# Edge one-hot columns with the block as the innermost dimension, read by TensorE with a step

## The reference, cut to what matters

```python
def _L0_gnn_ref(x, rots, idx_i, idx_j):        # rots: 100000 angles, idx_j sorted
    def step(mat, t):                           # one rotation of two rows, in order
        i, j, theta = t
        c, s = cos(theta), sin(theta)
        mat = mat.at[i].set(c * mat[i] - s * mat[j])
        mat = mat.at[j].set(s * mat[i] + c * mat[j])   # both from the rows before
    m = scan(step, eye(256), (idx_i, idx_j, rots)).T
    return x @ m

xn = _layernorm(x)                              # x: 6250 x 256
x = x + _L0_gnn_ref(xn, edge_weight, src, dst) + _L0_mix_ref(xn[None], ...)[0]
x = x + _L0_ffn_ref(_layernorm(x)[None], ...)[0]    # 8 experts, the best 2 per row
```

## Time and profile before

| | |
|---|---|
| median of 3 runs | 734.21 us (733.88 to 734.66) |
| the profiled execution's own time | 737.21 us |
| its span, first to last instruction | 735.3 us |
| busy: PE, PEld | 644.6 us (88%), 551.3 us (75%) |
| busy: DVE, ACT, POOL | 472.9 us (64%), 449.9 us (61%), 388.6 us (53%) |
| mean granted TensorE clock | 0.928 |

### The profile page before, as it was taken

The page is one execution under the profiler, slowest core; times in us unless marked ns, Lnnn a source line. Parts: engine busy times, 40 slices in busy tenths (PEclk is TensorE's granted clock), DMA queues, the critical chain, the costliest instruction groups (busy, mean ns, idle before and its releaser), DMA issues.

```text
span 735.3 us, 18134 instructions
## 1 busy us (share of the span) xinstructions
PE 644.6 (88%) x4079; PEld 551.3 (75%) x4080; DVE 472.9 (64%) x1877; ACT 449.9 (61%) x1235; POOL 388.6 (53%) x532
## 2 busy tenths in 40 slices
PE   5789899754798998059999999899989999999996
PEld 4457577532687776048998999899979999999996
DVE  5797666699865799333544444344457777777775
ACT  6777666487234699336665666566656666666663
POOL 6104777145434177715776777323246656666554
PEclk8899999955599999569999999999999999999999
DMA  8830112246400477622443334222223333333332
GB/s 241 229 88 12 22 31 23 52 142 203 142 27 2 125 225 218 199 71 95 140 138 123 120 119 131 70 69 62 69 79 103 101 98 103 106 102 96 107 97 69
DMA packets 60873, 78.10 MB, mean 106 GB/s; under 512 B 15868, under 2 KB 49488, under 8 KB 60570
## 3 DMA queue, kind: packets, MB, share of 16 engines
q1 hardware_dynamic: 45703, 42.94, 21.0%
q0 software_dynamic: 14544, 34.11, 13.9%
q10 hardware_dynamic: 576, 0.54, 0.3%
HBM read 47.53 MB, written 31.53 MB: 108 GB/s over the span
## 4 chain that ended last, share of the span: by engine, by line
PE 67%; DVE 9%; issue 7%; DMA 5%; POOL 4%; ACT 4%; SPq 2%; DVEq 0%; POOLq 0%; ACTq 0%
PE banks L2716 22%; PE banks L2726 20%; PE banks L2324 5%; PE banks L2668 5%; PE banks L2303 4%; POOL send_d L903 3%; PE banks L2707 3%; DMA R<-in_edge_weight_dram 1%; DMA R<-send_d 1%; DMA out_dram<-R,dest_now 1%; PE banks L2314 1%; DVE R L1760 1%; PE banks L2429 1%; PE banks L2294 1%; PE banks L2419 1%
## 5 line engine op out<-in xcount | busy, mean ns | idle before, releaser
L2716 PE MATMUL banks<-R 128*128 128x128 f32 x1696 | 210.4, 278 | 3.6 <-ACT R L1288 3.5
L2716 PEld LDWEIGHTS banks<-R 128*128 128x128 f32 x1696 | 201.1, 194 | 4.6 <-ACT R L1288 4.5
L2726 PE MATMUL banks<-R 128*128 x848 | 200.4, 379 | 0.0
L1301 ACT ACTIVATE R<-banks,b1c 128x128 f32<-128x128 f32 x424 | 142.9, 363 | 54.2 <-PE banks L2716 53.8
L2726 PEld LDWEIGHTS banks<-R 128*128 128x128 f32 x848 | 153.1, 191 | 16.4
L1288 ACT ACTIVATE R<-banks,bet_c,gam_c 128x128 f32<-128x128 f32 x212 | 85.4, 453 | 114.8 <-PE banks L2707 112.3
L2211 DVE COPY R<-R 128x1024 f32 x106 | 74.3, 701 | 77.6 <-PE banks L2716 59.8
L903 POOL DMA_INDIRECT send_d<-R,slot_all x98 | 98.5, 1005 | 45.7 <-issue 40.6
L916 POOL DMA_INDIRECT first_d<-R,dest_now x54 | 61.0, 1130 | 94.4 <-DVE R L2216 79.4
L925 POOL DMA_INDIRECT R<-first_d,get_now x52 | 53.7, 1033 | 48.9 <-DVE get_now L2193 46.8
L916 POOL DMA_INDIRECT out_dram<-R,dest_now x52 | 63.3, 1217 | 29.8 <-issue 26.5
(11 more groups left out here) (553 smaller groups left out, 957.0 us busy)
## 6 DMA issues: line engine op xcount, KB each, us to landing
R<-send_d SPq DMA_DIRECT2D x106, 131.0 KB
R<-in_L_ffn_W_dram SPq DMA_DIRECT2D x16, 512.0 KB, 4.5
R<-in_x_dram SPq DMA_DIRECT2D x14, 512.0 KB, 4.6
R<-in_x_dram SPq DMA_DIRECT2D x5, 1024.0 KB, 12.4
send_d<-zrow SPq DMA_DIRECT2D x14, 131.0 KB, 5.2
send_d<-R,slot_all POOLq DMA_INDIRECT x98
erec_d<-R SPq DMA_DIRECT2D x1, 1400.0 KB
R<-in_L_ffn_b_dram SPq DMA_DIRECT2D x1, 1024.0 KB, 5.6
```

The costliest lines, as they stand in the source:

```text
L1301: last = nc.scalar.activation(hT[b][:, c, :], bank[2 + 2 * b + c // 2][:, (c % 2) * P:(c % 2 + 1) * P], ACT.Gelu, bias=b1c[:, bass.ds(e, 1 ...
L2716: last = mm(bank[2 + 2 * b + c // 2][:, (c % 2) * P:(c % 2 + 1) * P], w1c[b][:, kb, c * P:(c + 1) * P], xmT[b][:, kb * P:(kb + 1) * P], st ...
L2726: last = mm(bank[6 + b][:, 0:D], hT[b][:, c, :], w2s[:, bass.ds(e, 1), c, :].rearrange("p a h -> p (a h)"), start=(c == 0), stop=(c == H / ...
```

## The change

The one-hot columns are laid out with the block innermost, for each number a run of 26 (or 24) blocks, where before there was for each block a run of 128 (or 33) numbers. The first half now has 26 blocks and the second 24, where both had 25. POOL makes a constant `numbers16` of 128 x 26 bf16 on 125 partitions, which holds each number 26 times, in place of the row of 128; it is made at the same place of POOL's list by one copy from `col0` that reads each element 26 times. In the compares the blocks' ends are now read with a step of 1 innermost (and again for each number), and so are the constant and the output. The count of elements compared is as before. The matmuls read their operands with a step: for one block, 128 stationary columns and 33 (or 9) moving columns at a step of 26 elements (first half), 24 (second half) or 5 (head). The constant lies in R3, where the carving of the later tiles moves up by 1664 words; `col16` is gone from R1.

```diff
-        col16 = R1[0:EP, NT * D:NT * D + P // 2].bitcast(BF16)
+        numbers16 = prep(P, PB // 2 + PB // 2 % 2, dt=BF16, parts=EP)
...
-        half_c = PB // 2
+        half_c = PB // 2 + PB // 2 % 2
+        blocks_in = (half_c, PB - half_c)
...
         def cut_of(v, at, n, m):
-            return v[:, at:at + (n * m + 1) // 2].bitcast(BF16)[:, 0:n * m].rearrange("p (c n) -> p c n", c=n)
+            return v[:, at:at + (n * m + 1) // 2].bitcast(BF16)[:, 0:n * m].rearrange("p (n c) -> p n c", c=n)
...
-        hist_lo = [cut_of(t, 0, half_c, P) for t in tails]
-        hist_hi = [cut_of(t, at_hi, half_c, RC) for t in tails]
+        hist_lo = [cut_of(t, 0, m, P) for t, m in zip(tails, blocks_in)]
+        hist_hi = [cut_of(t, at_hi, m, RC) for t, m in zip(tails, blocks_in)]
...
-        def by_block(v, c0, c1, n, parts=EP):
-
-            return v[0:parts, c0:c1].rearrange("p (c a) -> p c a", a=1).broadcast_to([parts, c1 - c0, n])
...
-            link(nc.gpsimd.tensor_copy(col16[:, :], col0[0:EP, 0:P]))
+            link(nc.gpsimd.tensor_copy(numbers16, col0[0:EP, 0:P].rearrange("p (n c) -> p n c", c=1).broadcast_to([EP, P, half_c])))
...
             def hist_columns(h):
-                TT(hist_lo[h], by_block(ends_lo, h * half_c, (h + 1) * half_c, P), over_tiles(col16[0:EP, 0:P], half_c), ALU.is_equal).then_inc(S["edge_dve"], 1)
+                TT(hist_lo[h], over_tiles(ends_lo[:, h * half_c:h * half_c + blocks_in[h]], P), numbers16[:, :, 0:blocks_in[h]], ALU.is_equal).then_inc(S["edge_dve"], 1)
 
             def hist_rows():
                 for h in range(2):
-                    TT(hist_hi[h], by_block(ends_hi16, h * half_c, (h + 1) * half_c, RC), over_tiles(col16[0:EP, 0:RC], half_c), ALU.is_equal)
-                TT(head_lo, by_block(ends_lo, PB, PB + PH, P, HP), over_tiles(col16[0:HP, 0:P], PH), ALU.is_equal)
-                TT(head_hi, by_block(ends_hi16, PB, PB + PH, HC, HP), over_tiles(col16[0:HP, 0:HC], PH), ALU.is_equal).then_inc(S["edge_dve"], 1)
+                    TT(hist_hi[h], over_tiles(ends_hi16[:, h * half_c:h * half_c + blocks_in[h]], RC), numbers16[:, 0:RC, 0:blocks_in[h]], ALU.is_equal)
+                TT(head_lo, over_tiles(ends_lo[0:HP, PB:PB + PH], P), numbers16[0:HP, :, 0:PH], ALU.is_equal)
+                TT(head_hi, over_tiles(ends_hi16[0:HP, PB:PB + PH], HC), numbers16[0:HP, 0:HC, 0:PH], ALU.is_equal).then_inc(S["edge_dve"], 1)
...
                 for c in range(PH):
-                    mm(misc[:, P:P + HC], head_lo[:, c, :], head_hi[:, c, :], start=(c == 0), stop=(c == PH - 1))
+                    mm(misc[:, P:P + HC], head_lo[:, :, c], head_hi[:, :, c], start=(c == 0), stop=(c == PH - 1))
                 for c in range(PB):
-                    last = mm(misc[:, P + HC:P + NCH], hist_lo[c // half_c][:, c % half_c, :], hist_hi[c // half_c][:, c % half_c, :],
+                    last = mm(misc[:, P + HC:P + NCH], hist_lo[c // half_c][:, :, c % half_c], hist_hi[c // half_c][:, :, c % half_c],
                               start=(c == 0), stop=(c == PB - 1))
```

## The result

The changed kernel took 738.93 us in the median (737.7 to 741.28, 5 runs) against 734.21 us (732.23 to 734.66, 5 runs): +4.7 us between the medians. As a ratio it is 1.0069, 95% interval 1.0053 to 1.0086, which is +5.1 us (3.9 to 6.3). Slower was the forecast, with +1.8 us; the second interval reaches down to that, the first lies wholly above twice of it.

A forecast was written before the change was run, and what follows sets the result against it. PE was taken as the busiest engine, carrying the chain from 47.11 to 65.9 us. 0 (DVE) + 0 (POOL) + 1.8 (PE) on the 734.2 us median gave 736.0 us; own range 735.5 to 736.9, whole range 733.6 to 739.0.

The forecast's parts named there:

- The compares: DVE's histogram compares, 8735 elements per partition: 4.8 us shorter, none of it on the path, price 0.
- The constant: POOL's copy of 3328 elements in place of 128: about 2.7 us, hidden by slack behind it, price 0.
- The matmuls with a step: Histogram matmuls on PE: moving columns at 1.84 ns each, 61 ns per block against 25.4, +1.8 us for 50.
- The step that failed: Work behind the histogram, from the weighing at 57.40 on: moves later by the histogram's own added length.
- the weights that go column by column: Rival, histogram matmuls: stepped weights take 100 to 236 ns per block, +4 to +11.6 us, likely 738 to 740; chance 0.17.
- The hidden step: Rival, histogram matmuls: stepped reads hide under the 25.4 ns pace, time stays at 734.2 us; chance 0.28.
- DVE in the way: Rival, PE's gap before 47.11: the first compare's 1.6 us come off there, 732.6 us; chance 0.09.
- the slow copy: Rival, POOL's copy at 3.4 ns per element: tables 1.2 us late at 20.14, 735.4 to 737.2 us; chance 0.04.

The follow-up runs named there:

- the second interval: The changed kernel again, unaltered, in a second set of 12 runs against the kernel before: 1.0039 (1.0022 to 1.0056), +2.9 us (1.6 to 4.1).
- The pairs: Kernel before with each block's end stored twice, so compares run innermost over two neighbouring numbers, columns left in contiguous runs: 1.0008 (0.9987 to 1.0030).
- the probe: Kernel before plus twelve bursts of 30 unread matmuls on the constant at various steps: 25 ns per matmul contiguous, 66 ns with both operands at step 26.

## Why the prediction was wrong

*The compares.* Right in size and place: 4.5 us shorter (10.0 us to 5.5) against 4.8 forecast, and all of it turned into DVE's waits. The pairs show it without any step.

*The constant.* Right: 2.96 us against 2.7, though the slope for it was taken between two unlike copies, L711 with a step and L688 without. DVE's L1399 at 19.97 (L1402 before) is still released by the transfer, after 1.49 us of waiting. By the run with the constant alone it costs nothing.

*The matmuls with a step.* Right that the stepped reads set the pace, and close in size: 3.44 us against 3.05 for the 50. The value borrowed from DVE's rows, 1.84 ns per stepped element, was met to within 6% by TensorE's moving columns (1.7 to 1.8 ns). What I had left out is that the stepped weights come to 65 ns in the probe and 68 to 69 in the kernel, and so set the pace, a little above the 61 of the moving columns: 50 x 8 ns = 0.4 us. That the two operands cost nearly the same is luck; nothing in the prediction led to it.

*The step that failed* is the last one: "A later histogram therefore moves the whole of the rest by its own length." I took the granted clock of 1.00 in the earlier trace rows for a fixed property of the stretch and priced only the matmuls that were changed. The weighing behind them then ran at the lower level for 3.5 us, +1.7 us, nearly as much again as the step itself. The runs show that it follows a block that holds only stepped matmuls at this place: there in 4 of 4 traces, absent in 5 of 5 without such a block, among them one with the same length of contiguous matmuls, and absent in the one trace with the same stepped ones spread among dense ones. The mean clocks of the timed runs agree. What the chip measures to lower the clock is not shown here. The measured terms are then 2.2 us for the matmuls, where 1.8 was forecast, and 1.7 for the clock, where nothing stood. Together, 3.9 us, they lie at the edge of both intervals of the time, 3.9 to 6.3 and 1.6 to 4.1; the times alone don't prove the second term, and what the first result has beyond 3.9 us is open.

The measured 738.9 us lies outside the forecast's own range, 735.5 to 736.9. It lies at the very top of the whole one, 733.6 to 739.0, and by luck: that part was there for the weights that go column by column, at 738 to 740 us, which is not what happened.

*The rivals.* The hidden step fell: 25 ns held in the probe for contiguous operands and for weights at a step of 2, and for no other operands tried. Weights column by column fell: 65 ns, where that rival had 100 to 236. DVE in the way fell with the pairs, and the slow copy with the constant alone. The Trainium skill's page "TensorE: Matmul & The Clock Gate", section "Weight-path perf modes — Fast Weight Load (FWL) and DoubleRow", has the fast load take strided columns too. The trace agrees in so far as 128 stepped weights cost 0.5 ns each, though the pace with them is 2.6 times that of contiguous ones.

The rule of "Advanced Engine Details and Errata", section "SBUF Cachelines", in the Trainium skill points the right way. The probe's weights agree with it at 8 elements (16 bytes: 59 ns); at 4 elements (8 bytes, two to a line), where the rule has full rate, the weights pay already, 31 ns against 25, and 128 moving columns take 117 ns against 56.

## What to carry to other kernels

Keep the operands of small TensorE matmuls in contiguous runs: with a step of 16 bytes or more a moving column took 1.7 to 1.8 ns here and 128 weights 59 to 68 ns. When a stretch of matmuls is made slower, price the dense work behind it at the lower clock level as well: here that was 1.7 us beside 2.2. Slow matmuls spread among dense ones left the clock up, but no gain of time was shown for it. And time saved on an engine that waits is worth nothing until the order is changed to use it; a compare can get its step of 1 from pairs, without turning the layout over for the next engine.

## What was not expected of the hardware

Stepped weights and stepped moving columns cost the same together as the longer of them alone (66 ns against 65 and 60). A burst of stepped moving columns (128, at a step of 26) kept its 222 ns per matmul through a fall of the clock, and the next, at a step of 8, took 229 at the lower level. And two executions of one kernel put the clock's falls in different places (group 2's weighing at 5.41 and 3.72 us) while the pieces around it agree. A fall costs 1.7 us there; how much of the spread of about 5 us between runs of one kernel comes from such falls is open.
